# A mixture-of-experts and sparse-attention kernel: the one order of its stages is replaced by another

## The reference

```python
x = x + 0.5 * ffn(layernorm(x))      # 8 experts, top 2 of a softmax gate
x = x + attn(layernorm(x))           # per token only its 8 most similar earlier tokens
x = x + 0.5 * ffn(layernorm(x))      # the same weights once more

def ffn(x):                          # w1, w3: 8 x 512 x 256, w2: 8 x 256 x 512
    weights, idx = top_k(softmax(x @ gate_w.T), 2); weights /= weights.sum()
    h = silu(x @ w1[e].T) * (x @ w3[e].T)
    return sum(weights[k] * (h @ w2[e].T) for the two experts e)

def attn(x):                         # D_HEAD = 32
    A = the 8 largest of x @ x.T among earlier tokens
    p = softmax(where(A, (x @ W_q.T) @ (x @ W_k.T).T / sqrt(32), -1e9))
    return gelu((mix * x + (1 - mix) * (p @ x)) * gain + bias) * scale
```

## Time and profile before

| | us |
|---|---|
| median of 3 runs | 804.46 |
| lowest and highest run | 802.52, 806.79 |
| the profiled execution: its span, from the first to the last instruction | 805.24 |
| TensorE busy in it | 695.8 |
| VectorE, ScalarE, GpSimd busy | 561.3, 501.8, 451.6 |

### The profile page before, as it was taken

The page is one execution under the profiler, slowest core; times in us unless marked ns, Lnnn a source line. Parts: engine busy times, 40 slices in busy tenths (PEclk is TensorE's granted clock), DMA queues, the critical chain, the costliest instruction groups (busy, mean ns, idle before and its releaser), DMA issues.

```text
span 805.2 us, 17412 instructions
## 1 busy us (share of the span) xinstructions
PE 695.8 (86%) x4632; PEld 429.6 (53%) x4632; DVE 561.3 (70%) x1599; ACT 501.8 (62%) x975; POOL 451.6 (56%) x545
## 2 busy tenths in 40 slices
...
GB/s 337 426 221 162 116 211 179 164 134 143 170 206 126 180 159 149 199 160 172 168 171 197 173 192 168 149 186 135 186 158 178 162 201 144 128 164 212 236 246 320
DMA packets 318614, 150.75 MB, mean 187 GB/s; under 512 B 299133, under 2 KB 302589, under 8 KB 317757
## 3 DMA queue, kind: packets, MB, share of 16 engines
...
...
## 4 chain that ended last, share of the span: by engine, by line
PE 48%; DVE 18%; DMA 10%; issue 9%; ACT 6%; SPq 5%; POOL 3%; another core or an unknown queue 1%; POOLq 0%; ACTq 0%; DVEq 0%
PE B L1247 28%; PE B L1263 16%; DVE t_W L1557 2%; DMA yt<-t_W,t_idx 2%; DMA t_ph<-t_p 2%; DMA hs<-t_s,t_POS 2%; POOL hs L960 2%; DMA t_gh<-t_gp 2%; DVE t_s L1614 2%; DVE t_th L1755 1%; DMA t_W<-t_W 1%; PE B L1315 1%; PE B L1276 1%; SPq L1052 1%; DVE t_X L1775 1%
## 5 line engine op out<-in xcount | busy, mean ns | idle before, releaser
L1247 PE MATMUL B<-t_W,t_ht 128*128 x1704 | 398.9, 383 | 22.4 <-DVE t_W L1557 7.1
L1247 PEld LDWEIGHTS B<-t_W,t_ht 128*128 128x128 f16 x1704 | 166.8, 99 | 200.7 <-issue 35.8
L1755 DVE SCALAR_TENSOR_TENSOR t_th<-B,t_K,t_th 128x512 f32<-128x512 f32 x142 | 105.7, 747 | 115.9 <-PE B L1247 90.8
L1008 POOL DMA_INDIRECT yt<-t_W,t_idx x107 | 112.5, 1052 | 119.8 <-ACT t_W L1405 71.8
L1263 PE MATMUL B<-t_W,t_gh 128*128 x1284 | 160.7, 276 | 9.4 <-issue 6.4
L960 POOL DMA_INDIRECT hs<-t_s,t_POS x112 | 116.0, 1035 | 63.0 <-issue 29.0
L1263 PEld LDWEIGHTS B<-t_W,t_gh 128*128 128x128 f16 x1284 | 125.0, 99 | 43.2 <-issue 13.7
L1389 ACT ACTIVATE t_th<-B,t_K 128x512 f32<-128x512 f32 x142 | 96.8, 683 | 76.8 <-PE B L1247 49.1
L1398 ACT ACTIVATE t_gp<-t_th 128x512 f16<-128x512 f32 x107 | 66.2, 624 | 48.3 <-DVE t_th L1755 40.1
L1000 POOL DMA_DIRECT2D t_idx<-hs x142 | 80.1, 569 | 24.0 <-DMA yt<-t_W,t_idx 13.4
L1766 DVE TENSOR_TENSOR t_gp<-t_th,t_gp 128x512 f16<-128x512 f32 x107 | 75.0, 707 | 26.1 <-ACT t_gp L1398 21.3
...
## 6 DMA issues: line engine op xcount, KB each, us to landing
...
t_ht<-hs SPq DMA_TRANSPOSE x142
t_idx<-hs POOLq DMA_DIRECT2D x142, 0.5 KB
...
```

What stands on the lines that cost most here:

```text
L1008: eng.indirect_dma_start(yt_d[L], bass.IndirectOffsetOnAxis(ap=IDX[:, n % RING:n % RING + 1], axis=0), YO[n % YR], None).then_inc(d_y[n % ...
L1247: t = eng.matmul(B[b][:], HT[n % HTR][:, (2 * hl + db) * 128:(2 * hl + db) * 128 + 128], W16[:, bass.ds(expert[n] * 4096 + (db * 2048 + wl ...
L1755: eng.scalar_tensor_tensor(out=th[:], in0=B[b1][:], scalar=K[:, 7:8], in1=th[:], op0=ALU.mult, op1=ALU.mult).then_inc(free[b1], 1)
```

## The change

The string ORDER is another one; every other line is the same. The stages, their instructions, buffers and waits are those of before, and each string has 3121 stages. Of the string, which says nothing by itself, the first row of each is shown:

```diff
@@ -125,35 +125,35 @@
 ORDER = (
-    "))Bt)%)Bztf%efYeKY())BYY))BttLKL$$KLKL%$$++++qx%wpfeYKvY!!))fDLKL$$++eYYKLKL$++$Bt-^!!%f^!!e++>)q++xwp)Bt^+++++^"
...
+    "))B))Bt%tfz%eYfYe)(KLK$L$)Y)KYBLK$L$++)Bt%f))Bt1+eqxwpt%++fv!Y!!%D!-++YKfLKeYLe+^Y$$YKLKL^+^$!!:)$)Bt+qxw+!+V++Y"
...
```

More of the change, by code:

```diff
@@ L133 @@
[L133 to L137, removed]
@@ new lines @@
+    "%>++pvz$^!:))f=?B=u=se?!?Y=Y=??=!!=^^$t!!!)?=?=::W+%)B++fut$$?eqxw^!p%Y:_=fv?!1!1=^+++++!1e$Y~?!YYs1?==!W?=??=:$"
+    "^:z=?:^WW$?$u;q~!xw^=p!!.v=^s!;>W?=N??SP!;.;>WD-[;.;N>W=NSS=!?;.;>?QPh^;^P=?==;N!?|>.!!?;;N>SE!SQP;^h|PhW.NFVE^S"
+    ";!Q!QQP.>NF|EF;.|QSE*y1;WFhNu_*~~~~EWSFP>;.WM*;EN>;;*W_S~Qy1.N>Su;_*P;W>PFQ.;;N>S._cEWaNS~*~~;W;>FE_FW__;P.PQQ;."
+    "NSNS~E_F>*;PP.Q;NS>EWPQ;;FuW.>EQ~~*W;;P.NFNES}>*P;**;.Nu>QFQEF;WW*EF*;>;SS.PNSs.;N~~~*>EQF;WEF~P.PQ;>;SPNEFWuQ;S"
+    "Q~~~~.*>~~~**~EF;~~PE*~NQS.F*WP~_;QQNSEPFQHk>E;FE.F;>NEFRSPXy~WWuWW;;.N>;.;>**;NS*P*J;>S;PJW.NW;>;UUUS.QENQ~;>~W"
@@ new lines @@
+    "FSU;))Bt.EQNSP%;P.NPfeYIF>YSJJUUuUU));B;EFW>.Q;.EW*FTN**T;_>moPnSm~~o&t%n/WuNP;;f#<QS.QZWPG&iy/}N>EW;jF&#<E;*./&"
+    "eFQQY>;Zl#<WQGWuiZjGN/.#Y;lS><TdPTZiE~SFb;~j*;bECdmPGClNAF>onmi&Adoj.~S;n#/W&bN__EbP;/.Q<lZSFC*~<GbW#*diANPC>ZAj"
+    "QGEF&Q;O/ErFl;.#<i>))ENWS;&;***FQBZ>;j.EtPS%fPe/JJNlS#<U.dGWW;YYiQZ>;~~~d;:Q~~CFEU>PGb~U$jU*Nl.~;.);W:>;i)BtdSNF"
+    "EN*%fQPeS.j;b1>$Yl~;SFqY~***;WAxCTTAPQE.N~d>C1;QbCAwmuNoFWP;pWWvAnm*s!S.!&onP/>O<Nr~_~SSE#FP;u);>;).Z.GQ&NE*;/i^"
+    "<>;PF#jQZQ&WS^bN/lEGP;>;.iW!<!jNQ.#Z&S;SPFP#WdE>l;G/<iBNF;*tEjSC%.fJ>ZJu;U;FW~GEUlF*U_iNUP>b2_Q))jdB.dESb;QeW;Ny"
@@ new lines @@
+    ">.Ft*b*WQl;QCYSY~dPA.NS%feP*PE~;CA1NW:>;F*:QYA;>$$YSEC;A.;F~O~N*WTTqxwpv*PWr>uS.!E);;)m.oQQNWFBN!nmot>S^P&QuE%nf"
+    "PF/;Q_<#W;>;^eWY&Z.Y.EG/<i:W;F&#NSN!!>EjZPJ~~*SSJ#;*lG;F**/<PPQ~QZUGUUE~b~$FW.Q~&~~b1E>;U;)>.):iBNd#tS;%Ff$WjNe;"
+    "C>l/.YW*i~qS;P~dNEjPYx;.Fb><C*Z;wT;.ldGiTpNvNE*uAbCQQ_>j_lWSPFAmonmon&/<SE!!#FZ&G/<dCi#^;ZA&QWSjWG;>A^lP!P/OEFrd"
+    "i<.;&;))B!bN~>CQW.#E~t%S#j;feQP*;JFJEZlG/YNF*Y>:<UdbUU.;Z*:*iU)SE*N;Q)>$A$Bt.;jWqF*PQxbE;Sw%GNF*>Eubl.FSpvWEQPiW"
+    "dQjP;f!C1e;lFD>QEYC!N.;;F^Y.SA>E;^!~-NNSdTP.P;CFVT>!N*mSSPoPnmonQuAE&W;/AO.W;rWQ)>;;Fu*N<)B&S#/.t%<Ef>P#;JJWNU;&"
```

36 lines of the change are left out of this document (13 added, 23 removed).

## The result

The changed kernel takes 830.8 us, median of 4 runs (830.0 to 833.6), and the kernel before, on the same chip, 805.6 (802.5 to 806.9). The ratio is 1.0339, interval 1.0309 to 1.0369: slower by 3.4%, where 0.6% faster was forecast. The profiled execution has a span of 831.9 us against 805.2.

The account below looks back on a forecast made before the run. TensorE was taken to bound the middle, a VectorE and GpSimd chain the head. 805.2 - 9.4 (head) + 4.2 (middle) + 0.5 (end) = 800.5 us profiled, so 799.7 against 804.46; range 791.5 to 808.5.

Parts of the forecast that it names:

- The head: Start up to tile 9: earlier router places, table and gates start tile 9 at 133.7 us, not 143.1; gain 9.4 us.
- one block, gate, two blocks, `glow`, the table of 3.7 us (106 us): VectorE's work in the head, counted on from 96.3 us: the table done at 106 us, tile 3's gate at 112.
- The first bound for the head, 2.9 us: If gates come no sooner, only the put's wait and the slower `down` go, so the head gains just 2.9 us.
- The middle: TensorE's waits between head and end, summed from changed distances between producer and user: +4.2 us, bounds -4 and +11.4.
- `down` behind an eviction (L1263): TensorE's `down` directly behind another while one bank serves them: two close places wait about 2.1 us each, net +2.3.
- `msg` (L1315): TensorE's `msg` closer behind `sco`, mean 16.4 us instead of 18.9: two short places wait longer, +3.2 us.
- The slow rival: Probabilities reach TensorE later than `msg` asks, `msg` waiting 10.4 us more than before: 809.6 us, chance 0.13.
- `rank` (L1219, L1221): TensorE's router ranks: layer 1's first moves farther from its scores, saving 1.22 + 0.73 us; the last router's comes nearer, +1.3.
- there is no difference: TensorE's middle: summed work from `up` to `down` 21.7 us before, 22.0 now, and 5.4 for `up` in both orders.
- The end: Last tile's chain: joins ahead of the last `glow` hidden behind a put's landing, later stores +0.5 us, bounds 0 and 3.
- The rule of the lock: VectorE and GpSimd share a port pair: each scatter beside a weight block would wait up to a block's length.
- the rival built on that lock: Scatters stretched by VectorE's blocks, table not ready sooner, the head gains 2.9 us at most: 806.3 us, chance 0.17.

Follow-up runs that it names:

- e16: Changed kernel with TensorE's stages moved later at 13 places, other engines' programs kept, on a chip without late signals: 823.4 us, ratio 1.0386.
- e8: Kernel before with half the memory for the descriptors of GpSimd's DMAs, on a chip without late signals: 798.8 us, ratio 1.0104.
- e9: Changed kernel run again unaltered, on a chip with late signals: 831.7 us, ratio 1.0341 to the kernel before.
- e15: Changed kernel run again unaltered as a control, on a chip with late signals: 834.4 us, ratio 1.036 to the kernel before.
- e5: Changed kernel with 31 pauses on GpSimd ahead of densely packed indirect DMAs, on a chip without late signals: 811.0 us, ratio 1.0257 to the kernel before.
- e6: Kernel before with 12 pauses on GpSimd ahead of densely packed indirect DMAs, on a chip without late signals: 802.8 us, ratio 1.0119.
- e17: Kernel before with 12 GpSimd pauses and three more in the head, on a chip without late signals: 798.9 us, ratio 1.0073.
- e10: Kernel before run again unaltered for a profile, on a chip with late signals: ratio 1.0001.

## Why the prediction was wrong, step by step

**The head, forecast -9.4 us, measured +1.6.** The steps at which it can be read (us):

| | before | forecast | changed (A) | e16 (B) |
|---|---|---|---|---|
| first `up` | 90.4 | 90.4 | 92.0 | 88.9 |
| places of router 1 | 59.2 | 52.7 | 54.3 | 46.7 |
| places of router 2 | 81.4 | 77 | 77.5 | 74.4 |
| places of router 3 | 105.7 | 96 | 97.4 | 94.4 |
| gate of tiles 1 and 2 | 109.4 | (ahead of 112) | 115.7 | 103.4 |
| gate of tile 3 | 119.0 | 112 | 122.6 | 113.7 |
| last scatter | 137.0 | 126 | 132.7 | 126.0 |
| tile 9 | 143.1 | 133.7 | 144.7 | 135.6 |

The order does what I worked out from it. Up to 97 us the changed kernel keeps to the forecast within 1.6 us, and where no signal is late every later step is met too, within 2 us. On A the forecast breaks between 97 and 116 us, in the stretch shown above: the steps from the places of router 3 to the gate of tile 3 at 112 were summed from work on VectorE alone, as if the results of TensorE were there when done. They came up to 11.5 us late (100.38 to 111.90, the longest in any profile), while GpSimd started one scatter after the other, and with them the fast start of tiles was gone. The failed step is "one block, gate, two blocks, `glow`, the table of 3.7 us (106 us)": the table was done at 115.8. The same trace had the warning, the 5.67 us ahead of router 1 with "remote" behind it, and I passed over it as "one of full DMA load, and I leave it where it is". Nor is the whole gain that of the order: before's own head ends at 138.7 on B (e8), 4 us sooner than on A, so the order itself is worth 3 to 5 us there. On A tile 9 came between 142.5 (e9) and 146.9 us (e15) in the changed kernel, so that the +1.6 is itself good to some 2 us. One term was also summed wrongly: 48 scatters with 0.12 us more each are 5.8 us and not 3; on B the last scatter came at 126.0 all the same.

The first bound for the head, 2.9 us, was no bound: the head could lose, too.

**The middle, forecast +4.2 (-4 to +11.4), measured +23.4.** TensorE's waits, 145 to 800 us, of the changed kernel (us in total, times, longest):

```profile
PE B L1247 <- ACT t_th L1389: 6.5, 3, 3.1
PE B L1263 <- ACT t_W L1405: 6.2, 5, 2.2
PE B L1219 <- DVE t_ma L1656: 4.1, 3, 2.9
PE B L1221 <- DVE t_CP L1669: 3.0, 5, 1.4
PE B L1276 <- DMA t_hta<-t_s: 2.9, 3, 1.9
PE B L1247 <- DMA t_ht<-hs: 2.7, 2, 1.7
PE B L1209 <- DMA t_ph<-t_s: 2.7, 3, 1.4
...
PE B L1315 <- DMA t_ph<-t_p: 0.6, 1, 0.6
```

And of before:

```profile
...
PE B L1247 <- ACT t_th L1389: 3.3, 3, 1.5
PE B L1219 <- DVE t_ma L1656: 3.2, 2, 1.9
...
PE B L1263 <- ACT t_W L1405: 2.4, 3, 1.9
...
PE B L1315 <- DMA t_ph<-t_p: 1.7, 4, 0.7
...
PE B L1221 <- DVE t_CP L1669: 0.7, 1, 0.7
...
PE B L1209 <- DMA t_ph<-t_s: 0.5, 1, 0.5
PE B L1276 <- DMA t_hta<-t_s: 0.3, 1, 0.3
```

- `down` behind an eviction (L1263), forecast +2.3: +3.8. Right in kind. Part of it is late signals: `evict` itself waited 11.9 us for remote ones over the span.
- `msg` (L1315), forecast +3.2: by the DMA of probabilities it waits 1.1 us less than before, and by all its releasers together 2.3 against 1.7. The slow rival, which rested on `msg`, had its sign and not its mechanism.
- `rank` (L1219, L1221), forecast -1.95 and +1.3: +3.2. Distance in work did not become time; that the engines which feed it came late themselves is likely, but was not traced.
- What I had not looked at: `up` behind `tanh` +3.2, `up` behind its load +2.7, `qk` (L1276) +2.6, `score` (L1209) +2.2, and `sim` 0.2 to 1.5. These are 12 us, and the step that failed is the one that adds up work "over all `down`" and "all `up`" and finds "there is no difference". A mean distance says nothing of waits, which come at single places. On B, with pauses, in e5 it is these same kinds that lead (its L1228 is `score`, L1266 `up`, L1282 `down`, L1295 `qk`; 145 to 790 us), and so they are not only late signals:

```profile
PE B L1228 <- DMA t_ph<-t_s: 4.8, 4, 2.4
PE B L1266 <- DMA t_ht<-hs: 4.5, 3, 3.4
PE B L1282 <- ACT t_W L1424: 3.7, 4, 1.5
PE B L1295 <- DMA t_hta<-t_s: 3.4, 3, 1.8
```

Between 140 and 780 us TensorE's idleness was forecast at 27 us and measured 40.0 (22.9 before). From tile 9 to the last, 19.8 of the 23.4 us are idleness, and 3.6 us are a longer busy time. It is not the clock: the mean granted clock there is 0.995, and 0.993 before. TensorE stands for more than 0.15 us 43 times and not 30, and behind a wait the 12 matmuls of a `down` take 1.50 us, in a row 1.31; 13 such starts would be 2.5 us, an estimate. In the head and at the end the clock is lower than before (0.75 against 0.78, and 0.84 against 0.85) and TensorE is busy 1.9 and 1.3 us longer.

**The end, forecast +0.5 (0 to 3), measured +1.7**, 2.3 without late signals (29.8 in e5 and 27.1 to 27.8 in e8, e6 and e17), and 3.5 between e9 and e10 on one chip. At the upper bound, and with a wrong reason: I held the joins ahead of the last `glow` to be hidden behind the landing of tile 137's put. In the changed kernel TensorE waits for two `glow` in the last tiles:

```profile
811.04 0.62 PE L1185 MATMUL B<-t_identh,t_gp 128*128 128x128 f16 x8 [1.67 <-DVE t_gp L1766]
...
816.30 0.62 PE L1185 MATMUL B<-t_identh,t_gp 128*128 128x128 f16 x8 [2.02 <-DVE t_gp L1766]
```

**The rule of the lock.** The prediction set the lock of the Trainium skill (SBUF — State Buffer, "SBUF: two separate sides") against its sum. The head's 64 scatters have a mean of 1.07 us in the changed kernel and 1.10 before; most are 0.96 us, nine are 1.37 to 1.75. Those are tenths of microseconds against the 10 us by which the table missed its forecast; the rival built on that lock was not what happened.

**The range.** It was too narrow above since every bound in it was a bound on known waits. That an order replaced as a whole can make many small waits at places not looked at, and that one kind of wait in the trace ("remote") had no explanation, belonged into it. 831 us needs both.
